# A residual block of two 3x3 convolutions: the inner planes of conv 2 are rounded and split one by one, in another order on VectorE and ScalarE

## The chip, the cores and the metric

One Trainium2 chip, one of its cores. The metric is the device time of one execution in microseconds (us). The kernel before took 612.59 us in the median of three runs (612.04 to 614.04). Its profile is of one execution of 612.13 us, of which 610.5 us lie between the first and the last instruction.

## What is computed

`x` is 32 images of 64 channels of 56 x 56, float32. A residual block with inference batch norm:

```python
def _bn(x, gamma, beta, mean, var):
    inv = gamma * jax.lax.rsqrt(var + EPS)
    return x * inv[None, :, None, None] + (beta - mean * inv)[None, :, None, None]
identity = x
out = jax.nn.relu(_bn(_conv3x3(x, w1, stride=1), g1, b1, m1, v1))
out = _bn(_conv3x3(out, w2, stride=1), g2, b2, m2, v2)
return jax.nn.relu(out + identity)
```

## The kernel before

**The arithmetic.** The 128 partitions hold 64 channels of even rows and 64 of odd rows. Columns are also in two planes, even and odd, of 28. A 3-tap filter along the columns is computed for two output columns with four products instead of six (Winograd's F(2,3)): two "inner" products, of the sum and of the difference of the two column planes, and two "outer" ones, of differences of neighbours in one plane. The inner products are shared by both outputs: T1 and T2 are made in the banks `SUM_T1` and `SUM_T2`, then `join` writes T1 + T2 and T1 - T2 into the banks `EVEN` and `ODD`, on which the outer products are added.

**Rounding and splitting.** TensorE takes a rounded type (fp32r). Each plane is split: ScalarE copies it to `hi` in that type, VectorE computes `lo` = full - hi, and a product is hi x w_hi + hi x w_lo + lo x w_hi: three matmuls. For the hidden image of conv 2 the full planes are `t_inner` (two planes: sum and difference, 29 x 28 = 812 elements a partition each), the parts `ti_hi` and `ti_lo`, for the outer ones `t_outer`, `h_hi`, `h_lo`; for conv 1 `x_inner`, `x_outer`, `x_hi`, `x_lo`.

**Steps.** A step s works on three images at once: conv 1 of image s, the inner products of conv 2 of s - 1, the outer products of conv 2 of s - 2. `run` (L150) issues steps -1 to 33, the middle ones in a hardware loop of four. Each image is worked in two halves of rows; half 0 and half 1 have four PSUM banks each.

**The order is written out by hand,** one list per engine (`step` at L451, L594, L715), and an engine works its list strictly in that order. Semaphores hold an engine at an instruction until others are done. In a full step:
- TensorE: for each half, inner products of conv 1 of s, outer products of conv 2 of s - 2; then for each half, inner products of conv 2 of s - 1 (`inner_products_2`, L686), outer products of conv 1 of s. Each of these eight is 12 matmuls at L669. `inner_products_2` waits for `ti_lo` (`hlo_ready["inner"]`) and for `res_ready`. The inner products of conv 1 of s, half h, wait for join(2, s - 2, h).
- VectorE: join(2, s-2, 1); sum_hidden (L427) and difference_hidden (L433) of s - 1, which write t_inner; outer_hidden (L441); join(1, s, 0); split of the inner planes (L449, ti_lo); difference_x (L389); join(1, s, 1); outer_x (L396); split outer (L449, h_lo); split x inner (L404); join(2, s-1, 0); split x outer (L404).
- ScalarE: relu_hidden of s - 1, half 1 (L568, from PSUM into `hidden`); copy_sum(1, s, 0) (L562 and L563, from the T2 bank into `z`); high_hidden inner (L553, ti_hi); relu_out(s-2, 0) (L591, PSUM to `out_sb`); copy_sum(1, s, 1); residual(s-1, 0) (L543, x_inner into the T1 and T2 banks, two activations); relu_out(s-2, 1); high_hidden outer (h_hi); copy_sum(2, s-1, 0); residual(s-1, 1); high x inner (L533); relu_hidden(s, 0); high x outer; copy_sum(2, s-1, 1).
- The sync engine's queue loads x and the even planes and stores the output; GpSimd's queue adds the odd planes to `x_inner` by DMA.

`join(conv, n, half, before)` waits for copy_sum (`z_ready`), for the inner products and for what empties the EVEN and ODD banks: join(1, s, h) for relu_out(s-2, h) (`out_ready`), join(2, s-2, 1) for relu_hidden(s-1, 1) (`hidden_ready`). `residual(s-1, h)` waits for join(1, s, h), since it overwrites the T1 and T2 banks. relu_hidden waits for outer_hidden of the image before.

The last step (`is_step(s, N)`) has an order of its own, with the rows in two halves.

Of the kernel before, what the change touches and what calls it, by code (L numbers as in the profile page):

```python
# [7 lines left out]
ALU = mybir.AluOpType  # L8
# [16 lines left out]
def residual_block(nc, x, w1, w2, params, out):  # L25
    N, _, C, _ = x.shape
# [16 lines left out]
    with ExitStack() as ctx:  # L43
# [76 lines left out]
        xhi_ready = {"inner": sem("xhi_inner"), "outer": sem("xhi_outer")}  # L120
        xlo_ready = {"inner": sem("xlo_inner"), "outer": sem("xlo_outer")}

        th_ready = {"inner": sem("th_inner"), "outer": sem("th_outer")}
        hhi_ready = {"inner": sem("hhi_inner"), "outer": sem("hhi_outer")}
        hlo_ready = {"inner": sem("hlo_inner"), "outer": sem("hlo_outer")}

        inner = {1: sem("inner1"), 2: sem("inner2")}
        z_ready = {1: sem("z1_ready"), 2: sem("z2_ready")}
# [133 lines left out]
        def hidden_parts(which, b, half=None):  # L262

            rows = hidden_rows(half)
            if which == "inner":
                return t_inner[:, :, rows], ti_hi[:, :, rows], ti_lo[:, :, rows]
            return t_outer[:, :, rows], h_hi[:, b, :, rows], h_lo[:, b, :, rows]

        def before_conv2(n):
# [92 lines left out]
        def _(dve):  # L362
# [58 lines left out]
            def sum_hidden(n, half=None):  # L421

                rows = hidden_rows(half)

                dve.wait_ge(hidden_ready, 2 * n + (2 if half is None else half + 1))
                wait(dve, hlo_ready["inner"], n)
                nc.vector.tensor_tensor(t_inner[:, 0, rows], hid_data[:, 0, rows, 0:WQ], hid_data[:, 1, rows, 0:WQ],  # L427
                                        ALU.add)

            def difference_hidden(n, half=None):  # L430

                rows = hidden_rows(half)
                nc.vector.tensor_tensor(t_inner[:, 1, rows], hid_data[:, 1, rows, 0:WQ], hid_data[:, 0, rows, 0:WQ],  # L433
                                        ALU.subtract).then_inc(th_ready["inner"], 1)

            def outer_hidden(n, half=None):

# [13 lines left out]
            def step(s, k):  # L451
                ahead, now, last = there_is(s, s + 1), there_is(s, s), there_is(s, s - 1)
                ka, kl = (k + 1) % 4, (k + 3) % 4
                if is_step(s, N):

                    sum_hidden(N - 1, 0)
                    difference_hidden(N - 1, 0)
                    outer_hidden(N - 1, 0)
                    split_hidden("inner", N - 1, kl % 2, 0)
                    sum_hidden(N - 1, 1)  # L460
                    difference_hidden(N - 1, 1)
                    join(2, N - 2, 1, before_conv2(N - 2))
                    split_hidden("outer", N - 1, kl % 2, 0)
                    outer_hidden(N - 1, 1)
                    split_hidden("inner", N - 1, kl % 2, 1)
                    join(2, N - 1, 0, before_conv2(N - 1))
                    split_hidden("outer", N - 1, kl % 2, 1)
                    return

                if there_is(s, s - 2):  # L470
                    join(2, s - 2, 1, before_conv2(s - 2))
                if last:
                    sum_hidden(s - 1)
                    difference_hidden(s - 1)
                    outer_hidden(s - 1)
                if now:
                    join(1, s, 0, (2, s - 2))

                if last:
                    split_hidden("inner", s - 1, kl % 2)  # L480
                if ahead:
                    difference_x(s + 1, ka)
                if now:
# [21 lines left out]
        def _(act):  # L505
# [41 lines left out]
            def high_hidden(which, n, b, half=None):  # L547
                full, hi, _ = hidden_parts(which, b, half)

                act.wait_ge(th_ready[which], n + 1 + (half or 0))  # L550

                wait(act, *((inner[2], 4 * n) if which == "inner" else (outer[2], 2 * (n - 1))))
                nc.scalar.activation(hi, full, ACT.Copy).then_inc(hhi_ready[which], 1)  # L553

            def copy_sum(conv, n, half):
# [38 lines left out]
            def step(s, k):  # L594
                ahead, now, last = there_is(s, s + 1), there_is(s, s), there_is(s, s - 1)
                ka, kl = (k + 1) % 4, (k + 3) % 4
                if is_step(s, N):

                    residual(N - 1, kl, 0)
                    high_hidden("inner", N - 1, kl % 2, 0)  # L600
                    relu_hidden(N - 1, 1)
                    high_hidden("outer", N - 1, kl % 2, 0)
                    relu_out(N - 2, 0)
                    copy_sum(2, N - 1, 0)
                    high_hidden("inner", N - 1, kl % 2, 1)
                    residual(N - 1, kl, 1)
                    high_hidden("outer", N - 1, kl % 2, 1)
                    relu_out(N - 2, 1)
                    copy_sum(2, N - 1, 1)
                    return  # L610
# [11 lines left out]
                if now:  # L622
                    copy_sum(1, s, 0)
                if last:
                    high_hidden("inner", s - 1, kl % 2)
                if there_is(s, s - 2):
                    relu_out(s - 2, 0)
                if now:
                    copy_sum(1, s, 1)
                if last:  # L630
                    residual(s - 1, kl, 0)
                if there_is(s, s - 2):
                    relu_out(s - 2, 1)
                if last:
# [19 lines left out]
        def _(pe):  # L654
# [31 lines left out]
            def inner_products_2(n, half, more=0):  # L686


                pe.wait_ge(hlo_ready["inner"], n + 1 + more)
                pe.wait_ge(res_ready, 2 * n + half + 1)  # L690
                sum_products(2, half, 2, SUM_T2, passes_of(2, 2, 0), True).then_inc(inner[2], 1)
                sum_products(2, half, 1, SUM_T1, passes_of(2, 1, 0), True).then_inc(inner[2], 1)
# [89 lines left out]
```

## Time and profile before

| | before |
|---|---|
| median of 3 runs | 612.59 us |
| profiled execution | 612.13 us, span 610.5 us |
| TensorE, matmuls busy | 570.0 us (93%) |
| TensorE, weight loads busy | 553.2 us (91%) |
| VectorE busy | 549.7 us (90%) |
| ScalarE busy | 487.7 us (80%) |
| DMA | 131 GB/s over the span |
| mean granted TensorE clock | 0.991 |

The shares are averages over the whole span. Matmuls are pipelined: each lasts some 0.34 us in the profile while the next starts 0.18 us behind it. So where TensorE pauses is seen in the idle times ahead of single weight loads (engine PEld), which the timeline gives in brackets. Instructions of VectorE and ScalarE also overlap their followers a little: the next one starts before the end that the profile gives for the one before.

### The profile page before, as it was taken

How to read it: one execution, taken by the hardware profiler on the slowest of the kernel's cores; microseconds unless marked ns; L12 is line 12 of the kernel's file. 1: busy time of each engine (PE TensorE's matmuls, PEld its weight loads, DVE VectorE, ACT ScalarE, POOL GpSimd, SP SyncE). 2: the span in 40 equal slices, each digit the busy share in tenths (PEclk: the TensorE clock that was granted, in tenths of full speed). 3: DMA queues.
4: the chain of work that ended last, by engine and by line, in shares of the span. 5: the costliest groups of instructions: out<-in, count | busy, mean ns of one | idle time of the engine just before them, and what ended most of it. 6: DMA issues, size and time to landing. Idle time of an engine off the chain costs nothing.

```text
span 610.5 us, 8987 instructions
## 1 busy us (share of the span) xinstructions
PE 570.0 (93%) x3090; PEld 553.2 (91%) x3090; DVE 549.7 (90%) x443; ACT 487.7 (80%) x730; POOL 47.9 (8%) x52
## 2 busy tenths in 40 slices
PE   6769999999999999999999999999999999999997
PEld 3669999999999999999999999999999999999997
DVE  4699999999999999999999999999999999999974
ACT  4687789887788887787987778888778888778785
POOL 6700000000000000000000000000000000000000
PEclk9789999999999999999999999999999999999999
DMA  8444455435445444445443445534444534440112
GB/s 296 104 85 135 140 159 156 136 95 149 138 135 161 138 114 125 135 135 162 143 135 98 139 141 152 156 130 102 149 135 135 162 135 127 117 137 27 53 54 105
DMA packets 31679, 79.90 MB, mean 131 GB/s; under 512 B 2608, under 2 KB 19120, under 8 KB 31664
## 3 DMA queue, kind: packets, MB, share of 16 engines
q1 hardware_dynamic: 26912, 66.11, 29.9%
q0 software_dynamic: 4608, 13.31, 14.2%
q10 hardware_dynamic: 144, 0.29, 0.2%
q8 instruction: 9, 0.15, 0.1%
q14 instruction: 6, 0.05, 0.0%
HBM read 54.01 MB, written 25.69 MB: 131 GB/s over the span
## 4 chain that ended last, share of the span: by engine, by line
PE 56%; DVE 15%; issue 12%; ACT 12%; DMA 1%; POOL 0%; DVEq 0%; ACTq 0%
PE psum L669 56%; DVE ti_lo L449 9%; ACT out_sb L591 4%; DVE t_inner L433 3%; ACT hidden L568 3%; ACT z L563 2%; ACT z L562 2%; DVE t_inner L427 1%; ACT ti_hi L553 1%; DMA x_inner<-x_dram 1%; DVE psum L418 1%; ACT x_hi L533 0%; POOL w_mat L218 0%; DVE x_lo L404 0%; ACTq L560 0%
## 5 line engine op out<-in xcount | busy, mean ns | idle before, releaser
L669 PE MATMUL psum<-x_hi,w_hi 128*128 128x392 f32 (+2 forms) x512 | 176.3, 344 | 9.2 <-DVE x_lo L404 9.2
L669 PE MATMUL psum<-x_hi,w_lo 128*128 128x392 f32 (+2 forms) x512 | 175.5, 343 | 0.0
L669 PE MATMUL psum<-x_lo,w_hi 128*128 128x392 f32 (+2 forms) x512 | 175.3, 342 | 0.0
L418 DVE TENSOR_TENSOR psum<-psum,z 128x784 f32<-128x784 f32 (+1 forms) x128 | 127.1, 993 | 40.8 <-ACT hidden L568 14.4
L669 PE MATMUL psum<-ti_hi,w_hi 128*128 128x392 f32 x256 | 90.6, 354 | 23.8 <-DVE ti_lo L449 23.8
L669 PEld LDWEIGHTS psum<-x_hi,w_hi 128*128 128x128 f32 x512 | 97.4, 190 | 10.5 <-issue 6.3
L669 PEld LDWEIGHTS psum<-x_lo,w_hi 128*128 128x128 f32 x512 | 97.2, 190 | 0.4
L669 PEld LDWEIGHTS psum<-x_hi,w_lo 128*128 128x128 f32 x512 | 97.2, 190 | 0.4
L553 ACT ACTIVATE ti_hi<-t_inner 128x1624 fp32r<-128x1624 f32 (+2 forms) x33 | 50.3, 1524 | 54.2 <-DVE t_inner L433 54.2
L669 PE MATMUL psum<-h_hi,w_hi 128*128 128x392 f32 x256 | 87.2, 341 | 0.0
L669 PE MATMUL psum<-h_lo,w_hi 128*128 128x392 f32 x256 | 87.2, 341 | 0.0
L669 PE MATMUL psum<-ti_lo,w_hi 128*128 128x392 f32 x256 | 87.2, 341 | 0.0
L669 PE MATMUL psum<-ti_hi,w_lo 128*128 128x392 f32 x256 | 87.0, 340 | 0.0
L669 PE MATMUL psum<-h_hi,w_lo 128*128 128x392 f32 x256 | 86.9, 340 | 0.0
L568 ACT ACTIVATE hidden<-psum 64x56 f32<-64x56 f32 (+2 forms) x128 | 61.2, 504 | 29.6 <-PE psum L669 29.2
L562 ACT ACTIVATE z<-psum,bias 128x392 f32<-128x392 f32 (+1 forms) x128 | 75.1, 587 | 5.8 <-PE psum L669 2.7
L669 PEld LDWEIGHTS psum<-ti_hi,w_hi 128*128 128x128 f32 x256 | 48.0, 188 | 33.9 <-DVE ti_lo L449 24.8
L563 ACT ACTIVATE z<-psum,bias 128x392 f32<-128x392 f32 (+1 forms) x128 | 75.7, 592 | 0.0
L330 POOL DMA_DIRECT2D x_inner<-x_dram x32 | 28.1, 887 | 485.5 <-DMA x_inner<-x_dram 485.5
L543 ACT ACTIVATE psum<-x_inner 128x392 f32<-128x392 f32 x128 | 59.2, 501 | 7.1 <-DVE psum L418 7.1
L404 DVE TENSOR_TENSOR x_lo<-x_inner,x_hi 128x1568 fp32r<-128x1568 f32 x32 | 57.1, 1783 | 3.5 <-ACT x_hi L533 3.5
L591 ACT ACTIVATE out_sb<-psum 128x784 f32<-128x784 f32 x64 | 52.1, 814 | 9.4 <-PE psum L669 8.6
(66 smaller groups left out, 829.3 us busy)
## 6 DMA issues: line engine op xcount, KB each, us to landing
x_sb<-x_dram SPq DMA_DIRECT2D x32, 814.0 KB, 4.8
out_dram<-out_sb SPq DMA_DIRECT2D x64, 392.0 KB, 2.8
x_inner<-x_dram SPq DMA_DIRECT2D x32, 406.0 KB, 3.2
x_inner<-x_dram POOLq DMA_DIRECT2D x32, 406.0 KB, 5.1
z<-w_dram ACTq DMA_DIRECT2D x1, 288.0 KB, 3.8
out_sb<-w_dram SPq DMA_DIRECT2D x1, 288.0 KB, 6.2
bn<-params_dram SPq DMA_DIRECT2D x1, 132.0 KB, 3.6
```

The lines of the kernel that those rows point to most:

```text
L330: pool.dma_start(x_inner[:, k, 0], odd, accum_op=ALU.add).then_inc(summed[k], 16)
L404: nc.vector.tensor_tensor(x_part(x_lo, k, places), full, x_part(x_hi, k, places).bitcast(F32), ALU.subtract).then_inc(xlo_ready[which], 1)
L418: nc.vector.tensor_tensor(psum[:, half, EVEN:ODD + 1, 0:width], t1, z[:, half, :, 0:width], ALU.add).then_inc(joined[conv], 1)
L433: nc.vector.tensor_tensor(t_inner[:, 1, rows], hid_data[:, 1, rows, 0:WQ], hid_data[:, 0, rows, 0:WQ], ALU.subtract).then_inc(th_ready["in ...
L449: nc.vector.tensor_tensor(lo, full, hi.bitcast(F32), ALU.subtract).then_inc(hlo_ready[which], 1)
L543: ins = nc.scalar.activation(psum[:, half, bank, 0:width].rearrange("p (j q) -> p j q", q=WQ), x_full("inner", k)[0][:, i, j0:j1], ACT.Cop ...
L553: nc.scalar.activation(hi, full, ACT.Copy).then_inc(hhi_ready[which], 1)
L562: nc.scalar.activation(z[:, half, 0, 0:width], t2, ACT.Identity, bias=bias[:, conv - 1:conv])
L563: nc.scalar.activation(z[:, half, 1, 0:width], t2, ACT.Identity, bias=bias[:, conv - 1:conv], scale=-1.0).then_inc(z_ready[conv], 1)
L568: return nc.scalar.activation(hid_data[rows, :, pairs, 0:WQ], sums[rows], ACT.Relu)
L591: nc.scalar.activation(out_sb[:, half], psum[:, half, EVEN:ODD + 1, 0:(j1 - j0) * WQ], ACT.Relu).then_inc(out_ready, 1)
L669: ins = nc.tensor.matmul(psum[:, half, bank, first:first + (j1 - j0) * WQ], w[:, i, far, :], moving, start=not onto and at == 0, stop=at = ...
```

## The change

The difference and the sum of the hidden image's column planes (called t1, the sum, and t2, the difference) get semaphores of their own, and each is rounded (`high_hidden`) and split (`split_hidden`) by an instruction of its own over 812 elements, where one instruction of 1624 elements stood. The orders in a full step are then:
- VectorE: sum_hidden; join(2, s-2, 1); difference_hidden; split t1; join(1, s, 0); split t2; outer_hidden; difference_x; join(1, s, 1); and the rest as before.
- ScalarE: relu_hidden(s-1, 1); copy_sum(1, s, 0); high t1; relu_out(s-2, 0); high t2; residual(s-1, 0); copy_sum(1, s, 1); relu_out(s-2, 1); and the rest as before.

In the last step each pair of inner planes becomes two instructions in place. TensorE's `inner_products_2` waits for both planes.

```diff
@@ -120,9 +120,8 @@
         xhi_ready = {"inner": sem("xhi_inner"), "outer": sem("xhi_outer")}
         xlo_ready = {"inner": sem("xlo_inner"), "outer": sem("xlo_outer")}
 
-        th_ready = {"inner": sem("th_inner"), "outer": sem("th_outer")}
-        hhi_ready = {"inner": sem("hhi_inner"), "outer": sem("hhi_outer")}
-        hlo_ready = {"inner": sem("hlo_inner"), "outer": sem("hlo_outer")}
+        th_ready, hhi_ready, hlo_ready = (
+            {which: sem(f"{what}_{which}") for which in ("t1", "t2", "outer")} for what in ("th", "hhi", "hlo"))
 
         inner = {1: sem("inner1"), 2: sem("inner2")}
         z_ready = {1: sem("z1_ready"), 2: sem("z2_ready")}
@@ -262,8 +261,9 @@
         def hidden_parts(which, b, half=None):
 
             rows = hidden_rows(half)
-            if which == "inner":
-                return t_inner[:, :, rows], ti_hi[:, :, rows], ti_lo[:, :, rows]
+            if which != "outer":
+                i = ("t1", "t2").index(which)
+                return t_inner[:, i, rows], ti_hi[:, i, rows], ti_lo[:, i, rows]
             return t_outer[:, :, rows], h_hi[:, b, :, rows], h_lo[:, b, :, rows]
 
         def before_conv2(n):
@@ -423,15 +423,16 @@
                 rows = hidden_rows(half)
 
                 dve.wait_ge(hidden_ready, 2 * n + (2 if half is None else half + 1))
-                wait(dve, hlo_ready["inner"], n)
+                wait(dve, hlo_ready["t1"], n)
                 nc.vector.tensor_tensor(t_inner[:, 0, rows], hid_data[:, 0, rows, 0:WQ], hid_data[:, 1, rows, 0:WQ],
-                                        ALU.add)
+                                        ALU.add).then_inc(th_ready["t1"], 1)
 
             def difference_hidden(n, half=None):
 
                 rows = hidden_rows(half)
+                wait(dve, hlo_ready["t2"], n)
                 nc.vector.tensor_tensor(t_inner[:, 1, rows], hid_data[:, 1, rows, 0:WQ], hid_data[:, 0, rows, 0:WQ],
-                                        ALU.subtract).then_inc(th_ready["inner"], 1)
+                                        ALU.subtract).then_inc(th_ready["t2"], 1)
 
             def outer_hidden(n, half=None):
 
@@ -456,28 +457,31 @@
                     sum_hidden(N - 1, 0)
                     difference_hidden(N - 1, 0)
                     outer_hidden(N - 1, 0)
-                    split_hidden("inner", N - 1, kl % 2, 0)
+                    split_hidden("t1", N - 1, kl % 2, 0)
+                    split_hidden("t2", N - 1, kl % 2, 0)
                     sum_hidden(N - 1, 1)
                     difference_hidden(N - 1, 1)
                     join(2, N - 2, 1, before_conv2(N - 2))
                     split_hidden("outer", N - 1, kl % 2, 0)
                     outer_hidden(N - 1, 1)
-                    split_hidden("inner", N - 1, kl % 2, 1)
+                    split_hidden("t1", N - 1, kl % 2, 1)
+                    split_hidden("t2", N - 1, kl % 2, 1)
                     join(2, N - 1, 0, before_conv2(N - 1))
                     split_hidden("outer", N - 1, kl % 2, 1)
                     return
 
+                if last:
+                    sum_hidden(s - 1)
                 if there_is(s, s - 2):
                     join(2, s - 2, 1, before_conv2(s - 2))
                 if last:
-                    sum_hidden(s - 1)
                     difference_hidden(s - 1)
-                    outer_hidden(s - 1)
+                    split_hidden("t1", s - 1, kl % 2)
                 if now:
                     join(1, s, 0, (2, s - 2))
-
-                if last:
-                    split_hidden("inner", s - 1, kl % 2)
+                if last:
+                    split_hidden("t2", s - 1, kl % 2)
+                    outer_hidden(s - 1)
                 if ahead:
                     difference_x(s + 1, ka)
                 if now:
@@ -549,7 +553,7 @@
 
                 act.wait_ge(th_ready[which], n + 1 + (half or 0))
 
-                wait(act, *((inner[2], 4 * n) if which == "inner" else (outer[2], 2 * (n - 1))))
+                wait(act, *((inner[2], 4 * n) if which != "outer" else (outer[2], 2 * (n - 1))))
                 nc.scalar.activation(hi, full, ACT.Copy).then_inc(hhi_ready[which], 1)
 
             def copy_sum(conv, n, half):
@@ -597,12 +601,14 @@
                 if is_step(s, N):
 
                     residual(N - 1, kl, 0)
-                    high_hidden("inner", N - 1, kl % 2, 0)
+                    high_hidden("t1", N - 1, kl % 2, 0)
+                    high_hidden("t2", N - 1, kl % 2, 0)
                     relu_hidden(N - 1, 1)
                     high_hidden("outer", N - 1, kl % 2, 0)
                     relu_out(N - 2, 0)
                     copy_sum(2, N - 1, 0)
-                    high_hidden("inner", N - 1, kl % 2, 1)
+                    high_hidden("t1", N - 1, kl % 2, 1)
+                    high_hidden("t2", N - 1, kl % 2, 1)
                     residual(N - 1, kl, 1)
                     high_hidden("outer", N - 1, kl % 2, 1)
                     relu_out(N - 2, 1)
@@ -622,13 +628,14 @@
                 if now:
                     copy_sum(1, s, 0)
                 if last:
-                    high_hidden("inner", s - 1, kl % 2)
+                    high_hidden("t1", s - 1, kl % 2)
                 if there_is(s, s - 2):
                     relu_out(s - 2, 0)
+                if last:
+                    high_hidden("t2", s - 1, kl % 2)
+                    residual(s - 1, kl, 0)
                 if now:
                     copy_sum(1, s, 1)
-                if last:
-                    residual(s - 1, kl, 0)
                 if there_is(s, s - 2):
                     relu_out(s - 2, 1)
                 if last:
@@ -686,7 +693,8 @@
             def inner_products_2(n, half, more=0):
 
 
-                pe.wait_ge(hlo_ready["inner"], n + 1 + more)
+                pe.wait_ge(hlo_ready["t1"], n + 1 + more)
+                pe.wait_ge(hlo_ready["t2"], n + 1 + more)
                 pe.wait_ge(res_ready, 2 * n + half + 1)
                 sum_products(2, half, 2, SUM_T2, passes_of(2, 2, 0), True).then_inc(inner[2], 1)
                 sum_products(2, half, 1, SUM_T1, passes_of(2, 1, 0), True).then_inc(inner[2], 1)
```

## Rows read from the trace of the kernel before

**Rows 1.** The page: busy times by engine, and TensorE's granted clock in 40 slices.
```profile
PE 570.0 (93%) x3090; PEld 553.2 (91%) x3090; DVE 549.7 (90%) x443; ACT 487.7 (80%) x730; POOL 47.9 (8%) x52
...
PEclk9789999999999999999999999999999999999999
```

**Rows 2.** The waits: engine, line, waited for; us, times, longest us.
```profile
ACT ti_hi L553 <- DVE t_inner L433: 54.2, 31, 1.8
...
PE psum L669 <- DVE ti_lo L449: 23.8, 31, 2.5
...
DVE psum L418 <- ACT hidden L568: 14.4, 30, 0.5
```

**Rows 3.** Timeline of weight loads: start us, duration us, idle before.
```profile
41.45 0.19 PEld L669 LDWEIGHTS psum<-ti_hi,w_hi 128*128 128x128 f32 x1 [2.73 <-issue]
...
59.58 0.19 PEld L669 LDWEIGHTS psum<-ti_hi,w_hi 128*128 128x128 f32 x1 [1.07 <-ACT psum L543]
...
313.17 0.19 PEld L669 LDWEIGHTS psum<-ti_hi,w_hi 128*128 128x128 f32 x1 [1.08 <-DVE ti_lo L449]
...
313.28 0.19 PEld L669 LDWEIGHTS psum<-ti_hi,w_lo 128*128 128x128 f32 x1
...
584.63 0.19 PEld L669 LDWEIGHTS psum<-ti_hi,w_hi 128*128 128x128 f32 x1 [1.01 <-DVE ti_lo L449]
```

**Rows 4.** Timeline of TensorE's matmuls in one step.
```profile
303.70 0.35 PE L669 MATMUL psum<-x_hi,w_hi 128*128 128x420 f32 x1
...
305.92 0.34 PE L669 MATMUL psum<-h_hi,w_hi 128*128 128x392 f32 x1
...
307.87 0.34 PE L669 MATMUL psum<-h_lo,w_hi 128*128 128x392 f32 x1
...
312.08 0.34 PE L669 MATMUL psum<-h_lo,w_hi 128*128 128x392 f32 x1
...
315.43 0.35 PE L669 MATMUL psum<-x_hi,w_hi 128*128 128x420 f32 x1
```

**Rows 5.** Timeline of VectorE, in the first full step and in this one.
```profile
48.28 0.97 DVE L418 TENSOR_TENSOR psum<-psum,z 128x784 f32<-128x784 f32 x1
...
305.03 0.98 DVE L418 TENSOR_TENSOR psum<-psum,z 128x784 f32<-128x784 f32 x1 [0.50 <-ACT hidden L568]
...
307.75 1.84 DVE L441 TENSOR_TENSOR t_outer<-hidden 128x1624 f32<-128x1624 f32 x1
...
310.32 1.04 DVE L418 TENSOR_TENSOR psum<-psum,z 128x840 f32<-128x840 f32 x1 [0.73 <-PE psum L669]
...
311.27 1.84 DVE L449 TENSOR_TENSOR ti_lo<-t_inner,ti_hi 128x1624 fp32r<-128x1624 f32 x1
...
320.02 0.97 DVE L418 TENSOR_TENSOR psum<-psum,z 128x784 f32<-128x784 f32 x1
```

**Rows 6.** Timeline of ScalarE in the same step and the next.
```profile
307.95 1.57 ACT L553 ACTIVATE ti_hi<-t_inner 128x1624 fp32r<-128x1624 f32 x1 [1.84 <-DVE t_inner L433]
...
309.42 0.80 ACT L591 ACTIVATE out_sb<-psum 128x784 f32<-128x784 f32 x1
...
311.40 0.92 ACT L543 ACTIVATE psum<-x_inner 128x392 f32<-128x392 f32 x2 [0.23 <-DVE psum L418]
...
330.61 0.82 ACT L591 ACTIVATE out_sb<-psum 128x784 f32<-128x784 f32 x1 [0.22 <-PE psum L669]
...
331.33 1.56 ACT L553 ACTIVATE h_hi<-t_outer 128x1624 fp32r<-128x1624 f32 x1
...
333.72 0.93 ACT L543 ACTIVATE psum<-x_inner 128x392 f32<-128x392 f32 x2
...
334.56 1.52 ACT L533 ACTIVATE x_hi<-x_inner 128x1568 fp32r<-128x1568 f32 x1
```

**Rows 7.** Groups by form: shapes, count, busy us, mean ns, idle before.
```profile
L449 DVE TENSOR_TENSOR ti_lo<-t_inner,ti_hi 128x840 fp32r<-128x840 f32 x1 | 1.0, 1033 | 0.0
...
L553 ACT ACTIVATE ti_hi<-t_inner 128x840 fp32r<-128x840 f32 x1 | 0.9, 908 | 0.1
```

## The prediction

> **What bounds the kernel now.** I read the page first. TensorE is busy 93% of the span, VectorE 90%, ScalarE 80%, and from the fourth slice on the granted clock never leaves its top digit, the 2.4 GHz level [rows 1]. So the room is in TensorE's pauses, not in its speed. The list of waits names them [rows 2]: VectorE's `ti_lo` (L449) holds TensorE for 23.8 us in 31 waits. Ahead of it ScalarE waits 54.2 us for `t_inner` before it can round (`ti_hi`), and VectorE 14.4 us for `hidden` before join(2).
>
> Third, the timeline of the weight loads: one pause per step, at the inner products of conv 2, of 1.04 us or so [rows 3]. From the hold at 59.58 to that at 584.63 there are 29 steps, so a step is 525.05 / 29 = 18.105 us. A held start catches up 0.07 us (the second weight load comes 0.11 us behind the first, 313.17 to 313.28, instead of 0.18), so a hold costs 0.97 us and an unheld step would be 18.105 - 0.97 = 17.13 us.
>
> Fourth, one step from its first matmul at 303.70 (call this 0). TensorE runs eight blocks of 12 matmuls: A inner conv 1 half 0; B outer conv 2 half 0; C, D the same for half 1; E inner conv 2 half 0; F outer conv 1 half 0; G, H the same for half 1. A takes 2.22 us [rows 4]. B's last matmul ends at 307.87 + 0.34 = 308.21, so at 4.51. D's last starts at 312.08, so E is due at 312.26 (8.56) and its weight load at 312.08, but starts at 313.17, when `ti_lo` is done (311.27 + 1.84 = 313.11) [rows 3 to 5]. F starts at 315.43, 2.15 after E's start of 313.28 (313.17 - 0.07 + 0.18).
>
> The chain behind the hold, back from there: ti_lo stands on VectorE behind join(1, s, 0) (310.32); that one waited for out_sb, which ScalarE gave at 309.42 + 0.80 = 310.22; ScalarE gave it that late because the one big `ti_hi` (307.95) stood in front, though B had ended at 308.21; and ti_hi could not start before both hidden planes' combinations were there, after join(2), sum and difference (305.03 to 307.75 and 0.09 more) [rows 5, 6]. Check: 1.33 (the ReLU of `hidden` and its signal) + 2.81 + 0.11 is ti_hi at 4.25; + 1.47 + 0.80 + 0.10 + 0.95 + 1.84 = 9.42 against the due time 8.38. That is the hold.
>
> **The change, part by part.** (1) *ti_hi and ti_lo in two.* ScalarE: 840 elements took 0.91 us, 1624 took 1.57 (next start 1.47 later), so 812 take 0.88, next start 0.79 later: 0.11 us more per step, beside ScalarE's idle fifth [rows 1, 6, 7]. VectorE: 840 of ti_lo took 1.03, so 812 take 1.00; a follower starts 0.08 before its forerunner's end (join: 1.04 long, next start 0.95 later), so 0.92. Two times 0.92 against 1.76 is 0.08 us more [rows 5, 7]. (2) *Sum ahead of join(2, s-2, 1).* It starts when relu_hidden is done, at 1.33. join(2) ends at 3.3 instead of 2.3; who waits for it is C, whose weight load is due at 4.17, so this costs nothing with 0.9 us to spare. (3) *t1 rounded alone.* t1 is there at 2.4, ScalarE is free of copy_sum(1, s, 0) by then, so high t1 runs 2.5 to 3.4, in what is idle time now; VectorE splits it 4.15 to 5.07. (4) *relu_out(s-2, 0) no longer behind the big rounding.* It starts at B's end, 4.55, takes 0.82, and join(1, s, 0) starts at 5.46 (0.10 behind its end, as today) instead of 6.62 [rows 5, 6]. (5) *t2.* high t2 runs 5.25 to 6.13 behind relu_out, split t2 6.41 to 7.40. E needs it at 8.38: the hold is gone with 1.0 us to spare. residual(s-1, 0), moved ahead of copy_sum(1, s, 1), waits for join(1, s, 0): 6.54 to 7.46, also in time; copy_sum follows to 8.4, before D's end (8.73) brings the next relu_out, so nothing stands behind it. (6) *outer_hidden moved behind split t2.* It ends at 9.16; its reader, h_hi on ScalarE, cannot start before relu_out(s-2, 1) is through at 9.47, so it is hidden by 0.2 us. No DMA is added. The stores go out up to 1.2 us earlier against TensorE, the x loads keep their place behind outer_x and the residual; the first of these has a whole step before its reader, so I take nothing for SP and POOL (bounds -0.1 and 0.1 us a step). The added semaphores and TensorE's second wait: 0 to 0.05 us a step, taken as 0, as the wait on t1 is long over.
>
> **What is late next.** Two chains come to the front.
> a) D's end to G. In the next step, relu_out(s-2, 1) waited for D and started at 330.61 (I put this 0.03 behind D's last matmul, an estimate, as for B), then h_hi at 331.33, residual(s-1, 1) at 333.72 for 0.93: done 4.07 us after D's end [rows 6]. G's weight load is due 4.03 after it: 2.15 for E and 2.22 for F from D's last start, less the 0.34 that this matmul lasts [rows 4]. G is held by 0.04 us. Today the hold at E covers this.
> b) B's end to the next A. A waits for join(2, s-1, 0), the last but one instruction of VectorE's step. From join(1, s, 0) to join(2, s-1, 0) VectorE now takes 320.02 - 310.32 = 9.70 without a pause, seven instructions from the one start to the other [rows 5]. In the new order half of ti_lo stands before it (-0.84) and outer_hidden behind it (+1.76), and with its own 0.97: 11.59. So it ends at 5.46 + 11.59 = 17.05, and the next A's weight load, 0.18 ahead of A, waits for that: a step of 17.23.
> b) is a cycle, so the step is max(17.13 + 0.04, 17.23) = 17.23 us. VectorE's own work is today's 18.105 less its two pauses (0.50 and about 0.70, each 0.08 longer from the time a follower could have started), so 16.75, + 0.08 = 16.83: under 17.23 [rows 5].
>
> The sum: 29 steps x (18.105 - 17.23) = 25.4. The last full step has no next A to be held: 0.97 - 0.04 = 0.9. In the first (a hold of 2.73 until 41.45) VectorE works without a pause; join(2, 0, 0), today done at 48.28 + 0.97 = 49.25, comes 0.35 later by the extra instruction (0.08) and a wait for high t1 (0.27), 49.60, against 49.9 for the next A's weight load today (41.45 + 8.5, E to H): 0.3 gained, with 0 and 2.7 as bounds [rows 3, 5]. The tail after the last conv 1 is paced by TensorE in both orders; there each ti pair also becomes two and is done at about the same time: 0 (bounds -0.3, +0.3). Together 26.6 us. The profiled execution took 612.13 (span 610.5 and 1.6 around it); 612.13 - 26.6 = 585.5. The median of the runs is 612.59, 0.46 more, so I forecast 586.0.
>
> **A rule against it.** The row: a split costs VectorE 0.08 us, and it is at 16.83 of 17.23 us afterwards. The Trainium skill, Perfetto Trace Analysis, Optimizing Scalar/DVE Operations, says that each instruction carries a fixed access cost (it gives some 60 ns on VectorE) and that fewer, larger operations are better on a saturated engine, while smaller ones help where an unsaturated engine leaves holes in another. By its figure VectorE would be at 16.81, so the sum is the same; if VectorE counts as saturated the rule speaks for the rival V below, if not for the forecast.
>
> **The rivals.**
> N: *TensorE is never held.* The 0.10 us of b) is within what my readings of starts can be off. Step 17.13, 29 x 0.975 + 1.3 = 29.6: 583.0. For: both chains miss by 0.1 or less. Against: both come out late, none early.
> W: *One more wait in b).* High_x inner ends on ScalarE 5.50 after D's last matmul (334.56 + 1.52 - 330.58, D ending at 8.72), at 14.22, + 0.1, and VectorE comes to its split at 14.37: 0.05 us of room [rows 6]. split t2 has 0.18 us over high t2. Each us lost there is a us of the step. With 0.3 lost (the mean of the small waits of ScalarE and VectorE on each other, 0.2 to 0.5 [rows 5, 6]): 17.53, 29 x 0.575 + 1.2 = 17.9: 594.7.
> V: *VectorE becomes the bound with its pauses whole.* It pauses for relu_hidden (0.58 with the follower's 0.08) and now before join(1, s, 0) (5.46 - 5.07 = 0.39) [rows 5]. If neither shrinks: 16.83 + 0.97 = 17.80, 29 x 0.305 + 1.2 = 10.0: 602.6. Against: both pauses are pinned to TensorE, so a late VectorE eats them.
> U: *It doesn't do what it says.* The hold is only renamed: E waits for the residual instead. Today the residual is done at 311.40 + 0.92 = 312.32, 0.24 past the due time [rows 6]. Within 0.3%: 612. Against: the residual itself moves up by a us.
> S: *join(1, s, 0) gets late.* It now stands behind split t1, so it hangs on high t1. If ScalarE got to high t1 only in the slot after relu_out (5.25 to 6.13), split t1 would end at 7.15 and join start there, 1.69 late; all of b) moves with it, step 18.92, 29 x 0.815 = 23.6 slower: 636. It is slower than before from a join 0.88 us late, so a high t1 that ends at 5.3 instead of 3.4. Against: in ScalarE's queue high t1 stands before relu_out, with an idle stretch around it.
>
> **How the numbers follow.** Forecast 0.57 (583.8 to 589 by itself), N 0.15, W 0.13, V 0.06, U 0.04, S 0.05. A measurement tells 0.3% (1.8 us) from no change. Faster: 0.91, same 0.04, slower 0.05. The range 582.4 to 594 holds the forecast, N and the near half of W, and leaves out the rest.
>
> **What would show it.** Right: no pause of TensorE at E; weight loads of A held by join(2) (L418) by about 0.1 us, and of G by `psum` (the residual) by 0.05 or less; a step of 17.2 us; ScalarE's wait for t_inner nearly gone, its waits for TensorE (out_sb) grown to about 1.1 us a step; join(1, s, 0) at 5.4 to 5.5 behind A; VectorE's pauses together 0.3 to 0.4 a step. Wrong: E still held by ti_lo; a step above 17.4, with VectorE waiting for ScalarE's x_hi or ti_hi (then W), or without a pause at all (then durations grew and my sum of VectorE's work is off).

## The result and the profile after

The changed kernel takes 589.72 us (median of 4 runs, 588.93 to 590.03) against 612.39 us before (612.04 to 614.04): a ratio of 0.9623, 95% interval 0.9603 to 0.9643, 22.7 us faster. The forecast was 586.0 us, its range 582.4 to 594. The profiled execution took 589.92 us, span 588.2; before it was 612.13, span 610.5.

The page after, busy times by engine and the granted clock (before: [rows 1]):

```profile
PE 569.0 (97%) x3090; PEld 551.9 (94%) x3090; DVE 551.6 (94%) x476; ACT 494.3 (84%) x763; POOL 46.3 (8%) x52
...
PEclk9789999999999999999999999999999999999999
```

TensorE's work is the same 569 to 570 us at the same clock; only the time between is gone. VectorE has 1.9 us more work, ScalarE 6.6 us, in 33 more instructions each. The waits after (engine, line, waited for: us in total, times, longest us):

```profile
...
ACT out_sb L595 <- PE psum L676: 48.6, 63, 2.1
PEld psum L676 <- issue: 15.3, 37, 6.7
ACT psum L547 <- DVE psum L418: 13.8, 31, 1.2
DVE psum L418 <- PE psum L676: 11.1, 24, 0.5
...
DVE psum L418 <- ACT hidden L572: 1.2, 1, 1.2
...
ACT ti_hi L557 <- DVE t_inner L427: 0.2, 1, 0.2
```

The 54.2 us in which ScalarE waited for t_inner and the 23.8 us in which TensorE waited for ti_lo [rows 2] are gone: the first is down to 0.2, the second has no row left. ScalarE now waits for TensorE, some 1.3 us a step ahead of relu_out of half 0 and 0.2 ahead of that of half 1 (48.6 us in all). What is left of TensorE's holds stands in the timeline of its weight loads, no longer at E but at A (310.72) and at G (323.76):

```profile
310.72 0.19 PEld L676 LDWEIGHTS psum<-x_hi,w_hi 128*128 128x128 f32 x1 [0.19 <-issue]
310.83 0.19 PEld L676 LDWEIGHTS psum<-x_hi,w_lo 128*128 128x128 f32 x1
...
323.76 0.19 PEld L676 LDWEIGHTS psum<-ti_hi,w_hi 128*128 128x128 f32 x1 [0.16 <-issue]
```

The weight load behind a held one follows after 0.11 us instead of 0.18, so 0.07 is caught up: the hold at A costs 0.12 to 0.13 us, that at G about 0.10. The profile names no releaser for so short a hold. It follows from the timelines of TensorE, VectorE and ScalarE:

```profile
297.63 0.34 PE L676 MATMUL psum<-h_lo,w_hi 128*128 128x392 f32 x1
...
311.02 0.35 PE L676 MATMUL psum<-x_hi,w_lo 128*128 128x420 f32 x1
```

```profile
299.01 1.04 DVE L418 TENSOR_TENSOR psum<-psum,z 128x840 f32<-128x840 f32 x1 [0.48 <-PE psum L676]
...
309.62 0.98 DVE L418 TENSOR_TENSOR psum<-psum,z 128x784 f32<-128x784 f32 x1
...
314.92 1.00 DVE L450 TENSOR_TENSOR ti_lo<-t_inner,ti_hi 128x812 fp32r<-128x812 f32 x1
316.40 1.04 DVE L418 TENSOR_TENSOR psum<-psum,z 128x840 f32<-128x840 f32 x1 [0.48 <-PE psum L676]
317.35 0.99 DVE L450 TENSOR_TENSOR ti_lo<-t_inner,ti_hi 128x812 fp32r<-128x812 f32 x1
```

```profile
298.08 0.83 ACT L595 ACTIVATE out_sb<-psum 128x784 f32<-128x784 f32 x1 [1.26 <-PE psum L676]
...
322.71 0.93 ACT L547 ACTIVATE psum<-x_inner 128x392 f32<-128x392 f32 x2
```

Block B's last matmul ends at 297.63 + 0.34 = 297.97, relu_out runs from 298.08 to 298.91 and join(1, s, 0) starts at 299.01: so the pause of 0.48 ahead of this join ends with relu_out, though the profile names TensorE. join(2, s-1, 0) ends at 309.62 + 0.98 = 310.60 and A's weight load follows at 310.72; the residual of the next step ends at 322.71 + 0.93 = 323.64 and G's weight load follows at 323.76. From join(1, s, 0) to join(2, s-1, 0) are 309.62 - 299.01 = 10.61 us: the prediction's 11.59 less the last instruction's 0.98. Over 29 steps the starts of join(1, s, 0) lie 17.361 us apart; before it was 18.108. That is 29 x 0.747 = 21.7 of the 22.2 us between the two profiled executions.

### The profile page after: what moved, and what is told of

The parts are those of the page before. It is cut to its first block, busy times and chain, and to the rows that moved or that the text cites. A ratio compares the mean times of both kernels' runs of the same rounds, so it can differ in the third digit from the quotient of the medians.

```text
span 588.2 us, 9134 instructions
## 1 busy us (share of the span) xinstructions
PE 569.0 (97%) x3090; PEld 551.9 (94%) x3090; DVE 551.6 (94%) x476; ACT 494.3 (84%) x763; POOL 46.3 (8%) x52
## 4 chain that ended last, share of the span: by engine, by line
PE 92%; ACT 1%; DVE 1%; DMA 1%; issue 1%; POOL 1%; ACTq 0%
PE psum L676 92%; DMA x_inner<-x_dram 1%; POOL w_mat L217 0%; DVE x_lo L404 0%; DVE t_outer L442 0%; ACT h_hi L557 0%; ACT x_hi L537 0%; ACT z L567 0%; DVE ti_lo L450 0%; POOL out_sb L190 0%; ACT z L566 0%; ACT out_sb L595 0%; ACT psum L547 0%; ACT ti_hi L557 0%; DVE psum L418 0%
## 5 line engine op out<-in xcount | busy, mean ns | idle before, releaser
L676 PE MATMUL psum<-x_hi,w_hi 128*128 128x392 f32 (+2 forms) x512 | 178.5, 349 | 9.9 <-DVE x_lo L404 9.9
L595 ACT ACTIVATE out_sb<-psum 128x784 f32<-128x784 f32 x64 | 52.9, 827 | 48.6 <-PE psum L676 48.6
L450 DVE TENSOR_TENSOR ti_lo<-t_inner,ti_hi 128x812 fp32r<-128x812 f32 (+2 forms) x66 | 64.1, 974 | 0.4 <-ACT ti_hi L557 0.4
L396 DVE TENSOR_TENSOR x_outer<-x_sb 128x1624 f32<-128x1624 f32 x32 | 61.2, 1911 | 0.0
L450 DVE TENSOR_TENSOR h_lo<-t_outer,h_hi 128x1624 fp32r<-128x1624 f32 (+2 forms) x33 | 59.2, 1794 | 0.4 <-ACT h_hi L557 0.4
```

The source lines that it names most:

```text
L396: nc.vector.tensor_tensor(x_outer[:], runs(cells, 0, XPLANE), runs(cells, 1, XPLANE), ALU.subtract).then_inc(tx_ready["outer"], 1)
L450: nc.vector.tensor_tensor(lo, full, hi.bitcast(F32), ALU.subtract).then_inc(hlo_ready[which], 1)
L595: nc.scalar.activation(out_sb[:, half], psum[:, half, EVEN:ODD + 1, 0:(j1 - j0) * WQ], ACT.Relu).then_inc(out_ready, 1)
L676: ins = nc.tensor.matmul(psum[:, half, bank, first:first + (j1 - j0) * WQ], w[:, i, far, :], moving, start=not onto and at == 0, stop=at = ...
```

## The experiments

All times are medians beside runs of the kernel before on the same chip (612.2 to 613.1 us). "Step" is the mean of the last 29 distances between starts of join(1, s, 0) in the run's trace. In c_diffx, d_both, m_xfirst and p_first the very last distance is shorter (17.02, 16.95, 16.63, 16.66) and pulls the mean down; the others there are 17.32 to 17.34, or 17.21 to 17.23.

| kernel | us | step | ratio to before, interval |
|---|---|---|---|
| the change | 589.72 | 17.36 | 0.9623 (0.9603 to 0.9643) |
| b_resid | 589.54 | 17.36 | 0.9622 (0.9607 to 0.9636) |
| c_diffx | 589.26 | 17.32 | 0.9620 (0.9603 to 0.9638) |
| d_both | 589.32 | 17.31 | 0.9623 (0.9607 to 0.9639) |
| e_split_only | 595.22 | 17.48 | 0.9714 (0.9694 to 0.9734) |
| f_order_only | 647.63 | 19.29 | 1.0566 (1.0545 to 1.0588) |
| g_extra_on | 615.15 | 18.24 | 1.0037 (1.0025 to 1.0050) |
| h_extra_off | 599.09 | 17.70 | 0.9774 (0.9755 to 0.9794) |
| m_xfirst | 585.92 | 17.20 | 0.9556 (0.9539 to 0.9573) |
| p_first | 585.13 | 17.21 | 0.9549 (0.9534 to 0.9564) |
| i_outer_back | 612.25 | 18.04 | 0.9995 (0.9984 to 1.0006) |
| q_outer_back_copy | 593.33 | 17.41 | 0.9671 (0.9652 to 0.9690) |
| a_waits | 589.16 | 17.34 | 0.9612 (0.9596 to 0.9628) |

**The change's parts alone.** e_split_only: separate instructions, the old order. Both edits here are shown against the kernel before.

```diff
-                    split_hidden("inner", s - 1, kl % 2)
+                    split_hidden("t1", s - 1, kl % 2)
+                    split_hidden("t2", s - 1, kl % 2)
...
-                    high_hidden("inner", s - 1, kl % 2)
+                    high_hidden("t1", s - 1, kl % 2)
+                    high_hidden("t2", s - 1, kl % 2)
```

> The planes t1 and t2 rounded and split by instructions of their own, but VectorE and ScalarE in the order of the kernel before. Theory, laid out as in the prediction: high t1 3.3 to 4.1, high t2 4.25 to 5.1, relu_out 5.04, join(1, s, 0) 5.97, split t2 done 8.84, against E's due time 8.38: E is held by 0.5 us, step 17.63, 612.4 - 29 x 0.475 - 0.5 = 598. So the split alone is worth some 14 of the 22.7 us. Rival, the order is what pays: 612.

595.22 us, 2.8 less than the theory's number and far from the rival's. E is held by 0.40 us in the weight loads, which costs 0.33, where 0.50 was laid out; 17.13 + 0.33 = 17.46 of the measured 17.48:

```profile
304.97 0.19 PEld L675 LDWEIGHTS psum<-ti_hi,w_hi 128*128 128x128 f32 x1 [0.40 <-issue]
```

f_order_only: the new order, the pair still one instruction.

```diff
+                if last:
+                    sum_hidden(s - 1)
                 if there_is(s, s - 2):
                     join(2, s - 2, 1, before_conv2(s - 2))
                 if last:
-                    sum_hidden(s - 1)
                     difference_hidden(s - 1)
-                    outer_hidden(s - 1)
                 if now:
                     join(1, s, 0, (2, s - 2))
                 if last:
                     split_hidden("inner", s - 1, kl % 2)
+                    outer_hidden(s - 1)
...
-                if now:
-                    copy_sum(1, s, 1)
                 if last:
                     residual(s - 1, kl, 0)
+                if now:
+                    copy_sum(1, s, 1)
```

> The kernel before with the new order, but both inner planes still rounded and split by one instruction: sum, join(2, s-2, 1), difference, join(1, s, 0), split of both, outer_hidden; ScalarE: high inner, relu_out, residual, copy_sum(1, s, 1). Theory: high inner runs 4.25 to 5.72, join(1, s, 0) starts at 6.64 as before, but now outer_hidden lies behind it: join(2, s-1, 0) is done at 6.64 + 12.43 = 19.07 and the step is 19.3: 612.4 + 29 x 1.19 = 647, slower than before. Rival, the order is worth the difference between split alone (595.2) and the change (589.7) by itself: 607.

647.63 us with a step of 19.29: the theory's number within 1 us. VectorE's timeline shows the place:

```profile
304.37 0.99 DVE L433 TENSOR_TENSOR t_inner<-hidden 128x812 f32<-128x812 f32 x1
307.85 1.04 DVE L418 TENSOR_TENSOR psum<-psum,z 128x840 f32<-128x840 f32 x1 [2.49 <-PE psum L669]
308.80 1.84 DVE L449 TENSOR_TENSOR ti_lo<-t_inner,ti_hi 128x1624 fp32r<-128x1624 f32 x1
310.56 1.84 DVE L441 TENSOR_TENSOR t_outer<-hidden 128x1624 f32<-128x1624 f32 x1
```

VectorE stands still for 2.49 us, and outer_hidden, which before filled this pause, now comes behind it. The order by itself is 35 us worse, the split by itself 17 us better, both together 22.7 better: the parts don't add.

**What sets the step of 17.36.** The theory was the prediction's chain b). g_extra_on and h_extra_off put the same instruction (784 elements of `w1_mat`, less themselves, into a spare tile; 0.88 us from start to start) at two places of VectorE's step.

```diff
+                nc.vector.tensor_tensor(spare_sb[:], part, part, ALU.subtract)
...
                     outer_hidden(s - 1)
+                    if not is_step(s, 1):
+                        extra()    # g_extra_on
...
                     join(2, s - 1, 0, before_conv2(s - 1))
+                    if not is_step(s, 1):
+                        extra()    # h_extra_off
```

> The changed kernel with one more VectorE instruction in each step from 2 on, a tensor_tensor of 784 elements into a spare tile (0.88 us from start to start), behind outer_hidden, so between join(1, s, 0) and join(2, s-1, 0). Theory: it lies on the cycle that holds A, so the step becomes 17.36 + 0.88 = 18.24: 589.7 + 30 x 0.88 = 616. Rival, only VectorE's total counts (16.83 + 0.88 = 17.71): 589.7 + 29 x 0.35 = 600.

> The same extra instruction, but behind join(2, s-1, 0), so outside the part of VectorE's step that A waits for. Theory: it first eats the pause before join(1, s, 0); what is left makes VectorE's own work the bound: 16.83 + 0.88 = 17.71, 589.7 + 29 x 0.35 = 600 (599 to 602). If position didn't count it would be as slow as with the extra instruction on the cycle; if only the cycle counted, 589.7.

615.15 and 599.09 us: steps of 18.24 and 17.70, as laid out (18.24, 17.71). In g_extra_on A is held by 0.98 us while the pause before join(1, s, 0) stays; in h_extra_off this pause is gone:

```profile
303.80 0.97 DVE L424 TENSOR_TENSOR psum<-psum,z 128x784 f32<-128x784 f32 x1
...
304.89 0.19 PEld L684 LDWEIGHTS psum<-x_hi,w_hi 128*128 128x128 f32 x1 [0.98 <-DVE x_lo L410]
```

```profile
310.57 1.04 DVE L424 TENSOR_TENSOR psum<-psum,z 128x840 f32<-128x840 f32 x1 [0.48 <-PE psum L684]
...
314.19 0.97 DVE L396 TENSOR_TENSOR spare_sb<-w_mat 128x784 f32<-128x784 f32 x1
```

```profile
302.83 1.02 DVE L424 TENSOR_TENSOR psum<-psum,z 128x840 f32<-128x840 f32 x1
...
314.32 0.95 DVE L396 TENSOR_TENSOR spare_sb<-w_mat 128x784 f32<-128x784 f32 x1
```

The first two lines are join(2, s-1, 0) and A's weight load; the profile names x_lo, an instruction just ahead, as A's releaser, but by the end times it is this join (303.80 + 0.97 = 304.77, and 0.12 to the weight load). VectorE's total is the bound only in h_extra_off (16.83 + 0.88 = 17.71 us of work in a step of 17.70); in the change it isn't: there 0.53 us of the step of 17.36 is VectorE's pause, so the rival V falls.

**Is G part of it?** b_resid takes away G's hold alone.

```diff
-                    copy_sum(2, s - 1, 0)
                     residual(s - 1, kl, 1)
+                    copy_sum(2, s - 1, 0)
```

> The changed kernel (589.7 us), with residual(s-1, 1) put ahead of copy_sum(2, s-1, 0) in ScalarE's full step. TensorE's short hold at G (0.16 us in its weight loads, some 0.10 us net) ends, since the residual is then 0.9 us earlier. Theory: the step is set by the cycle from B's end over VectorE's run to join(2, s-1, 0) and the next A; G is no part of it, so A is held longer by what G gains: step stays 17.36, 589.7 within 0.5. Rival, the holds add up: 29 x 0.09 = 2.6 us less, 587.1.

589.54 us, step unchanged: the rival (587.1) falls. The pauses at G are gone from the timeline of weight loads, and those at A have grown from about 0.19 to 0.28. A hold inside a longer cycle costs nothing.

**Shortening that cycle.** c_diffx, and d_both with b_resid's edit too:

```diff
+                if ahead:
+                    difference_x(s + 1, ka)
                 if now:
                     join(1, s, 0, (2, s - 2))
                 if last:
                     split_hidden("t2", s - 1, kl % 2)
                     outer_hidden(s - 1)
-                if ahead:
-                    difference_x(s + 1, ka)
```

> The changed kernel, with difference_x(s+1) ahead of join(1, s, 0) on VectorE, into the pause of 0.42 to 0.48 us in front of this join. Theory: the cycle over VectorE gets shorter by 0.88 us less the 0.3 to 0.4 by which the join starts later, so A isn't held any more; G is still held by 0.10: step 17.23, 585.8 (585 to 587). Rival, VectorE's amount of work sets the step: nothing changes, 589.7.

> Both edits, the residual ahead of copy_sum(2, s-1, 0) and difference_x ahead of join(1, s, 0). Theory: no hold of TensorE is left in a full step: 17.13 to 17.15 us, 29 x 0.22 = 6.4 less: 583.3 (582.5 to 584.5). Rival: another wait of about 0.1 us comes up and it stays at the 585.8 of the one edit.

Both missed: 589.26 and 589.32 us where 585.8 and 583.3 stood. The first number is that of c_diffx's rival, VectorE's amount of work; but VectorE's work is the change's 16.83 us, and m_xfirst below has the same work and a shorter step. The pause before join(1, s, 0) is filled, as meant, but the step is still 17.33. In d_both VectorE and ScalarE read:

```profile
307.48 1.79 DVE L404 TENSOR_TENSOR x_lo<-x_inner,x_hi 128x1568 fp32r<-128x1568 f32 x1 [0.23 <-ACT x_hi L537]
...
316.29 1.03 DVE L418 TENSOR_TENSOR psum<-psum,z 128x840 f32<-128x840 f32 x1
317.23 0.99 DVE L450 TENSOR_TENSOR ti_lo<-t_inner,ti_hi 128x812 fp32r<-128x812 f32 x1
318.14 1.84 DVE L442 TENSOR_TENSOR t_outer<-hidden 128x1624 f32<-128x1624 f32 x1
...
324.81 1.79 DVE L404 TENSOR_TENSOR x_lo<-x_inner,x_hi 128x1568 fp32r<-128x1568 f32 x1 [0.22 <-ACT x_hi L537]
```

```profile
320.02 1.57 ACT L557 ACTIVATE h_hi<-t_outer 128x1624 fp32r<-128x1624 f32 x1
321.49 0.90 ACT L547 ACTIVATE psum<-x_inner 128x392 f32<-128x392 f32 x2
322.32 0.57 ACT L566 ACTIVATE z<-psum,bias 128x392 f32<-128x392 f32 x1
322.80 0.58 ACT L567 ACTIVATE z<-psum,bias 128x392 f32<-128x392 f32 x1
323.27 1.51 ACT L537 ACTIVATE x_hi<-x_inner 128x1568 fp32r<-128x1568 f32 x1
```

From the split of x inner to the end of outer_hidden VectorE has no pause (12.50 us, and 0.04 to ScalarE), then ScalarE has none until x inner is rounded (4.76 us, and 0.03 back): 17.33 us, a cycle in which TensorE has no part. m_xfirst takes one piece out of it:

```diff
                     residual(s - 1, kl, 1)
-                    copy_sum(2, s - 1, 0)
...
                 if ahead:
                     high_x("inner", s + 1, ka)
+                if last:
+                    copy_sum(2, s - 1, 0)
```

> d_both, and on ScalarE high x inner ahead of copy_sum(2, s-1, 0). In d_both a cycle without TensorE was read: VectorE from the split of x inner (307.48) to the end of outer_hidden of the next step, then on ScalarE h_hi, residual, copy_sum, high x inner, 4.79 us, and back to the split of x inner (324.81), 17.33 us in all. Theory: the edit takes copy_sum's 0.94 us out of this cycle (16.4), so that TensorE's own 17.13 is the longest; 17.13 to 17.2, 29 x 0.13 to 0.2 = 3.8 to 5.8 less than d_both's 589.3: 583.5 to 585.5. Rival, VectorE cannot keep a step under 17.3 whatever the order (its waits are made up elsewhere): 589.

585.92 us, 3.4 less than d_both; the rival falls, the theory's 583.5 to 585.5 is just missed. The step is 17.22 to 17.23 (without its last distance), not 17.13. Its trace shows one more such cycle: ScalarE without a pause from h_hi at 301.67 to relu_hidden, VectorE without one from sum_hidden to outer_hidden, and h_hi again at 318.90, 17.23 us later:

```profile
301.67 1.57 ACT L557 ACTIVATE h_hi<-t_outer 128x1624 fp32r<-128x1624 f32 x1
...
309.61 1.01 ACT L572 ACTIVATE hidden<-psum 64x56 f32<-64x56 f32 x2
...
318.90 1.57 ACT L557 ACTIVATE h_hi<-t_outer 128x1624 fp32r<-128x1624 f32 x1
```

The halves meet without TensorE: relu_hidden starts 0.5 us behind the matmuls that it waits for, sum_hidden 0.03 behind relu_hidden, and h_hi 0.03 behind outer_hidden. This last cycle is read, not tested. p_first keeps difference_x in its old place in step 1 (`if ahead and not is_step(s, 1)`).

> m_xfirst with difference_x left in its old place in step 1 alone. There VectorE has no pause before join(1, 1, 0), so the early difference_x only delays it, the residual and the first E by 0.88 us. Theory: 0.7 to 0.9 us less, 585.1. Rival: the next hold takes it back, 585.9.

585.13 us, the number that was expected, and the fastest kernel here, 0.8% under the change. The intervals of p_first and m_xfirst overlap, so their times alone don't separate the two; in the traces the first two distances between the joins are 33.41 us in m_xfirst and 32.55 in p_first, 0.86 less.

**What moving outer_hidden is worth.** i_outer_back puts it back:

```diff
+                if last:
+                    outer_hidden(s - 1)
                 if now:
                     join(1, s, 0, (2, s - 2))
                 if last:
                     split_hidden("t2", s - 1, kl % 2)
-                    outer_hidden(s - 1)
```

> The changed kernel with outer_hidden back ahead of join(1, s, 0), where it stood before the change. Theory: join(1, s, 0) now stands behind 1.76 us more of VectorE's own work and starts at 6.74 instead of 5.57; split t2 is done at 8.69 against E's due time 8.38, so E is held by 0.3 to 0.35; A is not held (join(2, s-1, 0) is done at 16.6). Step 17.46 against 17.36: 589.7 + 29 x 0.1 = 592.6 (592 to 594). Rival, moving outer_hidden was only harm (it put 1.76 us on the part that A waits for): 17.23, 586.

612.25 us: both fall, and the whole gain is gone. ScalarE and VectorE of i_outer_back:

```profile
310.77 0.92 ACT L548 ACTIVATE psum<-x_inner 128x392 f32<-128x392 f32 x2 [1.58 <-DVE psum L418]
311.63 0.57 ACT L567 ACTIVATE z<-psum,bias 128x392 f32<-128x392 f32 x1
...
312.57 0.82 ACT L596 ACTIVATE out_sb<-psum 128x784 f32<-128x784 f32 x1
```

```profile
295.45 0.98 DVE L418 TENSOR_TENSOR psum<-psum,z 128x784 f32<-128x784 f32 x1 [0.96 <-ACT out_sb L596]
...
309.70 1.04 DVE L418 TENSOR_TENSOR psum<-psum,z 128x840 f32<-128x840 f32 x1
...
313.49 0.98 DVE L418 TENSOR_TENSOR psum<-psum,z 128x784 f32<-128x784 f32 x1 [0.96 <-ACT out_sb L596]
```

The late join (309.70) makes the residual late, and copy_sum and relu_out(s-2, 1) stand behind it on ScalarE; join(1, s, 1) waits for that relu_out. 313.49 - 295.45 = 18.04 us, once more without TensorE. q_outer_back_copy tests this reading by the order on ScalarE alone:

```diff
                     high_hidden("t2", s - 1, kl % 2)
-                    residual(s - 1, kl, 0)
                 if now:
                     copy_sum(1, s, 1)
+                if last:
+                    residual(s - 1, kl, 0)
```

> i_outer_back, which took 612.3 where 592.6 was expected, and on ScalarE residual(s-1, 0) back behind copy_sum(1, s, 1). Read from i_outer_back's trace: join(1, s, 0) starts 1.2 us later than in the changed kernel, residual(s-1, 0) waits for it, copy_sum(1, s, 1) and relu_out(s-2, 1) stand behind the residual, and join(1, s, 1) waits 0.96 us for that relu_out; from join(1, s, 1) on VectorE has no pause but 0.17 us until it is there again: a cycle of 18.04 us on VectorE and ScalarE. Theory: with copy_sum ahead of the residual this cycle is 0.94 us shorter (17.1), what is left is the hold at E until residual and split t2 are done (8.7 against 8.38): step 17.48, 593 (592 to 595). Rival, outer_hidden ahead of the join costs 22 us by itself: 611.

593.33 us: the theory's number. So with the change's order of residual and copy_sum, outer_hidden back in its old place costs 22.5 us; with these two exchanged as well, the kernel is 3 to 4 us slower than the change (3.6 by the medians).

**The two waits of relu_out.** In the change's trace relu_out of half 0 starts 0.114 to 0.119 us behind B's last matmul in the 24 steps of the hardware loop and 0.037 behind it in the steps that are written out behind the loop. The profiler's records of the waiting instructions show a difference: in the loop the wait for TensorE sits on a register instruction ahead of the activation (L147) and the wait for the old store on the activation; in the written-out steps it is the activation that waits for TensorE. a_waits exchanges the two waits.

```diff
-                act.wait_ge(outer[2], 2 * n + half + 1)
                 wait(act, stored[half], 16 * n)
+                act.wait_ge(outer[2], 2 * n + half + 1)
```

> The changed kernel with the two waits of relu_out in the other order: first the wait for the old store, then the one for TensorE. In the hardware loop the wait for TensorE (outer[2]) of half 0 sat on a register instruction that works out the value of the second wait, and relu_out started 0.12 us behind TensorE's last matmul; in the unrolled steps it is 0.04. Theory: it is 0.04 in all steps, the 24 steps of the loop come down from 17.38 to the unrolled 17.33: 1.2 us less, 588.5. Rival, the loop's longer step has another cause (17.31 in one of four steps): 589.7.

589.16 us; its interval overlaps the change's, so whether the time moved is not settled. The edit did not do in most steps what its theory took for granted: the activation itself waits for TensorE in one of four steps of the loop only; in the other three, and in all written-out steps, that wait now sits on a separate semaphore instruction. Over the relu_outs of the full steps in both traces, the start goes by where this wait sits:

| the wait for TensorE sits on | relu_out starts behind the last matmul |
|---|---|
| the activation | 0.036 to 0.037 us |
| a separate semaphore instruction | 0.096 to 0.097 us |
| a register instruction | 0.114 to 0.119 us |

In a_waits this also slows what was fast: relu_out of half 1 goes from 0.037 to 0.097 in three of four steps, and the written-out steps from 17.33 to 17.39. Why the exchanged waits land where they do is not shown.

## Why the prediction was right, and where it was off

1. *The hold at E and its chain* were right: it is gone, and so is ScalarE's wait for t_inner.
2. *The split's price*, 0.08 us on VectorE, was right: ti_lo's halves take 0.999 us in the mean of 62, with the follower 0.91 or 0.92 later where it has nothing to wait for. ScalarE's halves take 0.877 (0.88 laid out).
3. *sum_hidden ahead of join(2, s-2, 1)* cost nothing, and join(1, s, 0) was not late for it (S did not occur). VectorE's pause before it is 0.42 to 0.48 us in the profile, 0.50 to 0.56 from when a follower could have started; by that second measure 0.39 was laid out. The join starts 5.57 us behind A (316.40 - 310.83), where 5.4 to 5.5 was given; item 5 has the reason.
4. *What is late next*: both chains, a) at G and b) at the next A, are there, and b) is the one that counts: b_resid, g_extra_on and h_extra_off show it. Both holds are larger than the signs that were given for them: at A 0.12 to 0.13 us net (0.10 laid out), at G about 0.10 (0.04 laid out). Together with the unheld step they give the measured one, 17.13 + 0.13 + 0.10 = 17.36.
5. *The mis-sized term is b)*: 17.23 laid out, 17.36 measured, 29 x 0.13 = 3.8 us, which is the distance between 586.0 and 589.7. The run of VectorE was right to 0.01 (11.59). Off were the ends. relu_out starts 0.12 us behind B in the loop, not 0.03 to 0.04 (as it does behind D); I had taken this from other waits of ScalarE's. And from the end of join(2, s-1, 0) to the start of A the sum has 0.18 us, the distance from a weight load to its matmul, and nothing for the way from the join to the weight load. That way took 0.12 us, of which 0.07 is caught up again, so it is 0.22 to 0.23 us in three of four steps (310.60 to 310.83, where A would have started if its second matmul, at 311.02, had followed it unheld by 0.19) and 0.16 in the fourth; the distance behind that one is 17.32, the others are 17.38 to 17.39. In the written-out steps relu_out starts 0.04 behind B, but the join 0.13 behind relu_out's end instead of 0.10, and the step is 17.33.
6. *The first and the last steps* gave about 0.5 us, not 1.2. In the profiled execution after, TensorE's step 1 began at 33.27 instead of 32.93, ahead of any of the change's instructions, so 0.34 of it is the start of this run. In the profiled executions the forecast is off by 4.4 us (585.5 and 589.92): 3.7 from the steps and 0.7 from the first and last. That the medians differ by 3.7 only is chance: the profiled execution before lay 0.46 us under the median that the forecast started from, the one after lies 0.20 over its own.
7. *The rule on fixed costs*. The Trainium skill, Perfetto Trace Analysis, Optimizing Scalar/DVE Operations, says that breaking instructions up may let work be completed sooner where VectorE isn't saturated but causes pauses elsewhere. This case agrees: VectorE was busy 90% before and held TensorE once a step, and the split alone is worth 17 us (e_split_only). That grouping would be better on a VectorE that is full, as in h_extra_off, no run here shows.
8. *My own forecasts of the variants* failed where I followed one cycle only: c_diffx, d_both and i_outer_back were each held by a cycle over VectorE and ScalarE which the layout of the change's chain had not listed.

## What to carry to other kernels

The last cycle named here, of 17.23 us, is the one that no run tests; the others are. With engines that each work a fixed list, lay the lists beside each other and write down every cycle, from one instruction to itself a step later, the ones without the busiest engine too; the longest is the step, and a wait outside it, however visible, is worth nothing (taking away G's 0.16 us in b_resid gained nothing). A filler belongs ahead of a pause and off the cycle, and its place is worth as much as its length: the same 0.88 us cost 25 us at one place and 9 at another, and outer_hidden in its old place cost 22.5 us, of which exchanging two operations of another engine gave back some 19. Filling a pause pays only up to the next longest cycle (c_diffx, d_both). Splitting an instruction pays where its first half opens an earlier slot, and an order written for the split can be far worse without it (35 us here).

## What was not expected of the hardware

- The same activation starts 0.04, 0.10 or 0.12 us behind the same matmuls, by whether it waits for them itself or a semaphore instruction or a register instruction ahead of it does (the change and a_waits). The order of two waits in the source doesn't settle which it is.
- Holds of TensorE of 0.16 to 0.19 us cost less than they show: the weight load behind the held one comes after 0.11 us instead of 0.18 (306.36, 306.47 in the timeline of weight loads), as it did behind the holds of 1.04 us [rows 3].
